# A two-layer attention and mixture-of-experts kernel: additions in two blocks of eight tiles, token transposes ahead of their rows, and the normalisation of batch 2 moved behind six scatters

## The chip, the cores and the metric

The kernel runs on one core of a Trainium2 chip. The metric is the device time of the whole program in microseconds (us), measured over several executions. TensorE (PE) multiplies matrices, VectorE (DVE) and ScalarE (ACT) work on elements, GpSimd (POOL) does small arithmetic here and issues the indirect DMAs (scatters by a list of row numbers), and SyncE (SP) issues the plain DMAs. Each engine runs its own list of instructions in order, and they wait for each other through semaphores.

## What is computed

The reference has two layers over x, four sequences (batches) of 1024 tokens with 128 features, in float32:

```python
xn = _layernorm(x)
x = x + _L0_attn_ref(xn, ...) + _L0_ffn_ref(xn, ...)   # causal attention with rotary tables; top-1 of 8 experts
xn = _layernorm(x)
x = x + _L1_attn_ref(xn, ...) + _L1_ffn_ref(xn, ...)   # long convolution (FFT) with a filter; top-2 of 8 experts
```

In the second expert layer each token goes to its two best experts: `relu(xs @ W1[e] + b1[e]) @ W2[e] + b2[e]`, weighted by the softmax of the gate logits `xn @ Wg`.

## The kernel before

Tokens are cut into 32 tiles of 128 (NT = 32, J = 8 tiles a batch). The work comes in three parts.

**The rows.** The attention of layer 0 runs as a loop over the 32 query tiles, called rows 0 to 31; PE, ACT and DVE each have a loop of their own over n. In row n PE makes the scores of tile n+1 (`scores`), transposes the probabilities of tile n (`transpose_probs`), and multiplies those of tile n-1 by the values (`weigh_values`). ACT first copies the transposes out of PSUM (`take_pt`, L1002), then takes the exponentials of tile n+1 (`exp_rows`, L992). DVE takes the maximum of tile n+1 (`row_max`, L1729), and adds the weighted values of tile n-1 to the residual (`attention_row`, L1747). In rows 20 and 22 PE also makes the rotary projections of batch 3 (`project`), whose products DVE rotates (L1721, L1722, L1712). The two PSUM banks of scores are shared by scores and projections: the second projection of row 22 waits until the exponentials of tile 22 have emptied its bank.

Hung into rows 20 to 31 is the end of layer 0 and the beginning of layer 1. `add_tiles(first, end)` on DVE adds the rows of the first expert layer to the residual (L1763), and takes the statistics of the second normalisation (L1767, L1771); `ADD_BEFORE_MAX` and `ADD_BEHIND_ROW` say in which row, ahead of `row_max` or at the row's end. POOL makes the inverse deviations out of them (`inverse_std`, L811, L813) and the negated means (L873, L875). ACT normalises the tiles of batches 0 to 2 (`norm_rows`, L1009, rows in `NORM_AT`), DVE those of batch 3 (L1502). PE transposes the normalised tiles (`transpose_norms`, L1281, four at a time, unit u covers tiles 4u to 4u+3), ACT copies them to xT (`take_transposed`, L1014), PE multiplies them by the gate weights (`gates`) and ACT copies the logits (`take_gates`, L1018), all of it in the rows of `GATES_AT`. With the logits of batches 0 and 1, which are the first half, DVE runs the routing of that half (`routing1(0, ...)`, 30 steps, L1525 to L1596) in pieces, by `ROUTING_BEFORE_MAX` and `ROUTING_BEHIND_ROW`; the tables of slots that it ends in (L1592) start the scatters. In `COUNTS_AT` PE counts the tokens of each expert; two exponentials on ACT belong to it.

**The prelude.** After row 31, PE makes the projections of layer 1 (16 units `("vu", k)`), the transposes 6 and 7 of batch 3, its gates and counts, and the eight forward transforms of the first half; DVE normalises batch 3, runs the passes of the radix step (L640 to L691), the routing of the second half and the products of the spectra (L1841). The DVE list has, in this order: normalise tiles 28 to 31, ten passes, routing up to step 12, twelve passes, the rest of the routing, eight products.

**The rounds.** 40 rounds follow, one for each pair of expert tiles: PE multiplies the two tiles of the pair, DVE adds the bias into `ys` (L1892), ACT copies the expert's weights (L1037), POOL sends the pair's rows back (`send_back`, two indirect DMAs, L849). In rounds 0 to 3 and 8 to 11 PE makes inverse transforms as well, in 4 to 7 forward ones, and behind them the output projection of the convolution. The rows of a pair are loaded by SP into 15 buffers: `load_rows` of tile n waits until tile n-15 has been sent back. Between these loads, in the same queue, SP loads the matrices of the transforms (L756).

**POOL's list**, in order: the second normalisation of batches 0, 1 and 2; the 32 dispatches of the first half (`dispatch`, L826, an indirect DMA each), with the two halves of batch 3's inverse deviations at the dispatches of `NORM_IN_SCATTER`; `SCATTER_IN_PRELUDE` dispatches of the second half; then for each pair its two `send_back` and `SCATTER_PIECES` = 2 more dispatches until all 32 are out. After every second indirect DMA POOL waits until it has been issued.

Of the kernel before, what the change touches and what calls it, by code (L numbers as in the profile page):

```python
# [168 lines left out]
GATES_AT = (23, 24, 29)  # L169
NORM_AT = {22: [(0, 0), (0, 1)], 23: [(1, 0), (1, 1)], 27: [(2, 0)], 28: [(2, 1)]}  # L170
COUNTS_AT = 26
WARM_COUNTS, WARM_FILTER, WARM_GATES, WARM_SCORES, WARM_COUNTS_2 = 7, 7, 7, {24: 3}, 6
WARM_PROBS = {5: 4, 7: 3, 9: 3, 19: 7, 22: 6, 26: 3, 28: 14}
# [5 lines left out]
ADD_BEFORE_MAX = {21: (4, 8), 22: (12, 16), 25: (20, 24), 29: (24, 28), 31: (28, 30)}  # L179
ADD_BEHIND_ROW = {20: (0, 4), 21: (8, 12), 23: (16, 20)}  # L180
ROUTING_BEFORE_MAX = {25: 6, 27: 8}
ROUTING_BEHIND_ROW = {25: 6, 26: 10, 27: R1_STEPS}
# [46 lines left out]
SCATTER_IN_PRELUDE, SCATTER_PIECES = 12, 2  # L229
NORM_IN_SCATTER = (6, 14)  # L230
# [25 lines left out]
def two_layer_kernel(nc, x_in, cst_in, rope_in, fw_in, iv_in, pe_in, wqk_in, wvg_in, w0_in, b0_in,  # L256
# [3 lines left out]
    with ctx:  # L260
# [273 lines left out]
        for n in range(NT):  # L534
            T_USES += [("p", n, c) for c in range((n % J + 4) // 4)]
# [8 lines left out]
            if gates_at(n):  # L544
                g = GATES_AT.index(n)
                T_USES += [("t", 2 * g), ("t", 2 * g + 1)]
                O_USES.append(("g", g))
# [250 lines left out]
        def _(pool):  # L798
# [70 lines left out]
            for g in range(B - 1):  # L869
# [6 lines left out]

            pool.wait_ge(ids_done, 2)
            pool.wait_ge(xn_done, NT + NT // 2)
            pool.wait_ge(slots_filled[1], 16 * TILES1 // 8)
            pool.wait_ge(slot1_ready, 2)  # L880
            for i in range(HT):
                if i in NORM_IN_SCATTER:
                    inverse_std(2 * B - 1, J // 2 * NORM_IN_SCATTER.index(i), J // 2)
                dispatch(0, 0, i)
            for g in range(2):
                second_ids(0, g)
                pool.wait_ge(ids_done, 3 + g)
                for i in range(HT // 2 * g, HT // 2 * (g + 1)):
                    dispatch(0, 1, i)
# [25 lines left out]
        def _(act):  # L915
# [125 lines left out]
            for n in range(NT):  # L1041
                take_pt(n)
# [18 lines left out]
                if gates_at(n):  # L1061
                    g = GATES_AT.index(n)
                    for u in (2 * g, 2 * g + 1):
                        take_transposed(u, t_bank("t", u))
# [80 lines left out]
        def _(pe):  # L1145
# [177 lines left out]
            for n in range(NT):  # L1323
# [6 lines left out]
                if n in FILT_AT:  # L1330
                    filter_layer(FILT_AT.index(n))
                transpose_probs(n)
# [11 lines left out]
                if gates_at(n):  # L1344
                    g = GATES_AT.index(n)
                    for u in (2 * g, 2 * g + 1):
                        wait_emptied(pe, T_USES, T_AT[("t", u)])
                        transpose_norms(u, t_bank("t", u))
                    wait_emptied(pe, O_USES, O_AT[("g", g)])
                    if g == 0:  # L1350
                        keep_running(o_bank("g", g), WARM_GATES)
# [622 lines left out]
```

## Time and profile before

| | |
|---|---|
| time, median of 3 runs (lowest to highest) | 466.6 us (465.99 to 467.1) |
| time of the profiled execution | 466.87 us |
| its span, first to last instruction | 465.0 us |
| mean granted clock of TensorE in it | 0.938 of full |
| rows 20 to 31 in it | about 156 to 232 us |
| prelude | about 232 to 274 us |
| rounds | about 274 to 450 us |

The time around the span is 1.87 us. The lines of the page and of the timeline that are used below have a section of their own. In a timeline row stand the start, the duration, the engine, the line, the operation, what it writes and reads, its shape, the number of instructions merged in it, and in brackets the idle time of the engine ahead of it with the engine and line that ended it; "issue" there means that nothing in the profile shows what ended it.

### The profile page before, as it was taken

Reading aid. Unit: us, or ns where it says so; the run is one execution under the profiler, and the core shown is the slowest. Engines: PE = TensorE matmul, PEld = TensorE weight load, DVE = VectorE, ACT = ScalarE, POOL = GpSimd, SP = SyncE. Lnnn points to the kernel's source line nnn. Section 1 sums busy time; section 2 is a strip of 40 time slices with the busy share of each in tenths; the row PEclk is TensorE's granted clock in tenths of the full one; section 3 lists DMA queues with packets and bytes.
Section 4 is the critical chain, followed back from the end, with each engine's and each line's share of the span. In section 5 each row is a group of like instructions: output and inputs, shape, how many; then the busy total and the mean of one; then the engine's idle time right before and its main releaser. Section 6 shows DMA issues by size and latency. Waiting matters only on the chain.

```text
span 465.0 us, 7797 instructions
## 1 busy us (share of the span) xinstructions
PE 369.7 (79%) x2300; PEld 297.6 (64%) x2300; DVE 289.6 (62%) x786; ACT 224.0 (48%) x551; POOL 238.2 (51%) x246
## 2 busy tenths in 40 slices
PE   0686789959999978897996989899977969777800
PEld 0662246627779646755895879898866959676700
DVE  3956635945773498387579797489439991344106
ACT  1453144213434425436253236724757886788804
POOL 3401666524666322015666566666666666565640
PEclk9998989979999989889899899999999998999965
DMA  9999999228421340001101193454341222723407
GB/s 214 280 241 327 175 172 175 58 66 277 137 68 46 91 116 1 1 0 36 42 29 41 41 243 110 122 155 137 104 130 58 79 69 74 249 84 86 126 17 260
DMA packets 64744, 55.05 MB, mean 118 GB/s; under 512 B 6819, under 2 KB 56683, under 8 KB 64446
## 3 DMA queue, kind: packets, MB, share of 16 engines
q1 hardware_dynamic: 57888, 41.71, 37.0%
q0 software_dynamic: 6656, 12.51, 8.9%
q10 hardware_dynamic: 158, 0.33, 0.4%
q8 instruction: 19, 0.31, 0.3%
q14 instruction: 23, 0.19, 0.2%
HBM read 30.44 MB, written 25.27 MB: 120 GB/s over the span
## 4 chain that ended last, share of the span: by engine, by line
PE 45%; DVE 20%; issue 12%; ACT 7%; DMA 6%; POOL 5%; SPq 2%; ACTq 1%; another core or an unknown queue 1%; POOLq 0%; DVEq 0%
PE psS L1147 22%; PE psO L1147 14%; POOL slots L839 5%; PE psT L1147 4%; DMA slots<-row,slot 3%; PE psT L1263 2%; SPq L701 2%; ACT ring L1037 1%; DVE work L1841 1%; DVE work L1729 1%; ACT row L1009 1%; DMA work<-in_wvg 1%; DVE ys L1892 1%; ACTq L1036 1%; DVE work L1855 1%
## 5 line engine op out<-in xcount | busy, mean ns | idle before, releaser
L826 POOL DMA_INDIRECT slots<-row,slot x64 | 68.0, 1063 | 46.2 <-issue 27.9
L849 POOL DMA_INDIRECT moe<-ys,xs x61 | 62.7, 1028 | 47.5 <-issue 28.0
L1037 ACT ACTIVATE ring<-w 128x642 f32 x80 | 56.1, 741 | 40.9 <-DVE ys L1892 25.3
L839 POOL DMA_INDIRECT slots<-row,slot x32 | 35.1, 1096 | 37.5 <-DVE slot L1558 19.6
L1002 ACT ACTIVATE work<-psT 128x512 f32<-128x512 f32 (+3 forms) x32 | 16.5, 515 | 69.1 <-PE psT L1263 49.4
L849 POOL DMA_INDIRECT moe<-ys,w x35 | 35.7, 1021 | 19.6 <-issue 15.8
L1147 PE MATMUL psS<-work 128*128 128x512 f32 (+3 forms) x96 | 40.8, 537 | 3.2 <-ACT w L942 1.8
L1147 PE MATMUL psO<-work 128*128 128x128 f32 x288 | 39.0, 283 | 0.0
L992 ACT ACTIVATE work<-psS,work 128x128 f32<-128x128 f32 (+7 forms) x32 | 23.6, 738 | 30.2 <-DVE work L1733 28.1
L1729 DVE TENSOR_REDUCE work<-psS 128x1 f32<-128x128 f32 (+7 forms) x32 | 24.0, 749 | 21.1 <-PE psS L1147 19.3
L1147 PE MATMUL psS<-xT,work 128*128 128x512 f32 x64 | 32.7, 656 | 5.5 <-ACT work L992 5.5
L1147 PEld LDWEIGHTS psO<-work 128*128 128x128 f32 x288 | 36.4, 200 | 0.0
L1147 PE MATMUL psS<-xT,mats 128*128 128x256 f32 x128 | 29.8, 382 | 5.1 <-issue 3.8
L1147 PE MATMUL psT<-xsT,ring 128*128 128x128 f32 x160 | 22.3, 282 | 9.8 <-ACT xsT L1102 4.7
L1147 PEld LDWEIGHTS psS<-xT,mats 128*128 128x128 f32 x128 | 23.4, 190 | 9.3 <-issue 5.0
L1147 PE MATMUL psS<-work,mats 128*128 128x256 f32 x128 | 29.0, 382 | 0.2 <-DVE work L1841 0.2
L1892 DVE TENSOR_TENSOR ys<-psS,ring 128x256 f32<-128x256 f32 x20 | 8.5, 424 | 31.8 <-PE psS L1147 17.3
L1147 PEld LDWEIGHTS psS<-work 128*128 128x128 f32 x96 | 17.4, 204 | 16.3 <-issue 8.9
L1147 PEld LDWEIGHTS psT<-xsT,ring 128*128 128x128 f32 x160 | 19.4, 191 | 12.0 <-issue 6.3
L1263 PE MATMUL psT<-cst,work 128*128 128x128 f32 x144 | 22.9, 289 | 4.9 <-ACT work L992 4.6
L1147 PEld LDWEIGHTS psS<-work,mats 128*128 128x128 f32 x128 | 24.1, 193 | 3.7 <-issue 0.6
L1147 PE MATMUL psO<-xsT,ring 128*128 128x128 f32 x160 | 22.4, 283 | 4.7 <-ACT xsT L1102 2.6
(285 smaller groups left out, 842.7 us busy)
## 6 DMA issues: line engine op xcount, KB each, us to landing
slots<-xs SPq DMA_DIRECT2D x14, 516.0 KB, 12.5
mats<-in_iv SPq DMA_DIRECT2D x16, 256.0 KB
xs<-slots SPq DMA_DIRECT2D x61, 64.5 KB
w<-in_w SPq DMA_DIRECT2D x8, 321.0 KB
w<-slots SPq DMA_DIRECT2D x35, 64.5 KB
xres<-in_x SPq DMA_DIRECT2D x4, 512.0 KB, 9.6
moe<-xs SPq DMA_DIRECT2D x4, 512.0 KB, 9.2
mats<-in_fw SPq DMA_DIRECT2D x1, 2048.0 KB, 10.3
```

What stands on the lines that cost most here:

```text
L701: sp.dma_start(xres[:, J * g:J * (g + 1), :], xv[g]).then_inc(x_loaded[g], 16)
L826: pool.indirect_dma_start(slots1[:, :], bass.IndirectOffsetOnAxis(ap=(slot1, slot2)[k][:, i:i + 1], axis=0), row[:, i, :], None, bounds_ch ...
L839: pool.indirect_dma_start(dst[:, :], bass.IndirectOffsetOnAxis(ap=slots[:, i:i + 1], axis=0), row[:, i, :], None, bounds_check=bound, oob_ ...
L849: pool.indirect_dma_start(dst[:, :], bass.IndirectOffsetOnAxis(ap=row_slots[l][m][:, D:ROWW].bitcast(I32), axis=0), ys[:, n % UNROLL, :], ...
L992: act.activation(prob[n % 2][:, 0:(i + 1) * P], S[n % 2][:, :, :].rearrange("p a m -> p (a m)")[:, 0:(i + 1) * P], ACT.Exp, bias=negmax[:, ...
L1002: act.activation(pT[n % 2][:, 0:k, :].rearrange("p j q -> p (j q)"), t_bank("p", n, 0)[:, 0:k * P], ACT.Copy).then_inc(pt_act, 1)
L1009: act.activation(row[:, i, 0:D], xres[:, i, :], ACT.Identity, bias=nbias[:, i:i + 1], scale=rstd[:, i:i + 1]).then_inc(xn_done, 1)
L1037: act.activation(pair_w[p % RING_PAIRS][:, t, :], w12[:, bass.ds(e, 1), :].rearrange("p e h -> p (e h)"), ACT.Copy).then_inc(e_w, 1)
L1147: return pe.matmul(o, lhsT, rhs, start=start, stop=stop)
L1263: last = pe.transpose(t_bank("p", n, c)[:, (j - 4 * c) * P:(j - 4 * c + 1) * P], prob[n % 2][:, j * P:(j + 1) * P], ident)
L1729: dve.tensor_reduce(negmax[:, n:n + 1], S[n % 2][:, :, :].rearrange("p a m -> p (a m)")[:, 0:(n % J + 1) * P], X, ALU.max, negate=True).th ...
L1892: tt(ys[:, m:m + 2, :], out_bank(p).rearrange("p (t d) -> p t d", d=D), pair_w[p % RING_PAIRS][:, :, B2_AT:W_COLS], ALU.add).then_inc(e_ys ...
```

## The change

On DVE, tiles 0 to 7 are added in one block behind row 20 and tiles 8 to 15 in one block ahead of the maximum in row 21; before, they were four blocks of four, in rows 20 to 22. Tiles 16 to 23, which were in rows 23 and 25, go to rows 25 and 26. The gates of batches 0 and 1 move from rows 23 and 24 to rows 22 and 23, with their token transposes now ahead of `transpose_probs` on PE and their copies ahead of `take_pt` on ACT. The normalisation of batches 0 and 1 goes to the ends of rows 21 and 22, that of batch 2 to the end of row 28 in one piece. The routing of the first half is in rows 23 (12 steps), 24 (10) and 25 (the rest, ahead of the maximum). On POOL, the second normalisation of batch 2 stands inside the scatters, ahead of dispatch 6; the two halves of batch 3 ahead of dispatches 13 and 20 (were 6 and 14). Sixteen dispatches of the second half stand ahead of the first `send_back` (were 12). Four sets of matmuls that only keep PE busy are dropped: seven ahead of the first gates, six in row 22, three in row 26 and fourteen in row 28.

```diff
-GATES_AT = (23, 24, 29)
-NORM_AT = {22: [(0, 0), (0, 1)], 23: [(1, 0), (1, 1)], 27: [(2, 0)], 28: [(2, 1)]}
-COUNTS_AT = 26
-WARM_COUNTS, WARM_FILTER, WARM_GATES, WARM_SCORES, WARM_COUNTS_2 = 7, 7, 7, {24: 3}, 6
-WARM_PROBS = {5: 4, 7: 3, 9: 3, 19: 7, 22: 6, 26: 3, 28: 14}
+TOKENS_AT = (22, 23, 29)
+GATES_AT = (22, 23, 29)
+NORM_AT = {21: [(0, 0), (0, 1)], 22: [(1, 0), (1, 1)], 28: [(2, 0), (2, 1)]}
+COUNTS_AT = 24
+WARM_COUNTS, WARM_FILTER, WARM_SCORES, WARM_COUNTS_2 = 7, 7, {24: 3}, 6
+WARM_PROBS = {5: 4, 7: 3, 9: 3, 19: 7}
...
-ADD_BEFORE_MAX = {21: (4, 8), 22: (12, 16), 25: (20, 24), 29: (24, 28), 31: (28, 30)}
-ADD_BEHIND_ROW = {20: (0, 4), 21: (8, 12), 23: (16, 20)}
-ROUTING_BEFORE_MAX = {25: 6, 27: 8}
-ROUTING_BEHIND_ROW = {25: 6, 26: 10, 27: R1_STEPS}
+ADD_BEFORE_MAX = {21: (8, 16), 26: (20, 24), 29: (24, 28), 31: (28, 30)}
+ADD_BEHIND_ROW = {20: (0, 8), 25: (16, 20)}
+ROUTING_BEFORE_MAX = {25: R1_STEPS}
+ROUTING_BEHIND_ROW = {23: 12, 24: 10}
...
-SCATTER_IN_PRELUDE, SCATTER_PIECES = 12, 2
-NORM_IN_SCATTER = (6, 14)
+SCATTER_IN_PRELUDE, SCATTER_PIECES = 16, 2
+NORM_IN_SCATTER = (6, 13, 20)
...
+            second_norm(0)
+            second_norm(1)
...
+            def norms_in_scatter(j):
+
+                if j == NORM_IN_SCATTER[0]:
+                    second_norm(2)
+                if j in NORM_IN_SCATTER[1:]:
+                    inverse_std(2 * B - 1, J // 2 * (NORM_IN_SCATTER.index(j) - 1), J // 2)
...
+                if n in TOKENS_AT:
+                    g = TOKENS_AT.index(n)
+                    for u in (2 * g, 2 * g + 1):
+                        take_transposed(u, t_bank("t", u))
                 take_pt(n)
...
+                if n in TOKENS_AT:
+                    g = TOKENS_AT.index(n)
+                    for u in (2 * g, 2 * g + 1):
+                        wait_emptied(pe, T_USES, T_AT[("t", u)])
+                        transpose_norms(u, t_bank("t", u))
                 transpose_probs(n)
```

## Rows read from the trace of the kernel before

**Rows 1.** Page: busy time of each engine, and the group of dispatches.

```profile
PE 369.7 (79%) x2300; PEld 297.6 (64%) x2300; DVE 289.6 (62%) x786; ACT 224.0 (48%) x551; POOL 238.2 (51%) x246
...
L826 POOL DMA_INDIRECT slots<-row,slot x64 | 68.0, 1063 | 46.2 <-issue 27.9
```

**Rows 2.** Timeline of POOL: dispatches (L826) and send-backs (L849).

```profile
211.13 1.12 POOL L826 DMA_INDIRECT slots<-row,slot  x1 [11.38 <-DVE slot L1592]
...
234.07 0.23 POOL L811 TENSOR_SCALAR veps<-mv 128x4 f32<-128x4 f32 x1 [1.14 <-DVE mv L1771]
...
266.00 0.97 POOL L826 DMA_INDIRECT slots<-row,slot  x1 [0.78 <-issue]
...
286.29 0.97 POOL L849 DMA_INDIRECT moe<-ys,xs  x1 [1.26 <-issue]
...
326.15 0.97 POOL L849 DMA_INDIRECT moe<-ys,w  x1 [1.00 <-issue]
...
332.97 0.97 POOL L849 DMA_INDIRECT moe<-ys,w  x1 [0.78 <-DMA slots<-row,slot]
...
397.20 0.97 POOL L849 DMA_INDIRECT moe<-ys,xs  x1 [1.93 <-DVE ys L1892]
...
448.94 0.97 POOL L849 DMA_INDIRECT moe<-ys,xs  x1 [0.30 <-issue]
```

**Rows 3.** Timeline of SP's queue and of PE in rounds 9 and 10.

```profile
331.69 1.96 PE L1147 MATMUL psS<-xT,mats 128*128 128x256 f32 x8 [0.56 <-issue]
...
337.52 0.44 SPq L756 DMA_DIRECT2D mats<-in_iv  x1
...
340.63 1.97 PE L1147 MATMUL psS<-xT,mats 128*128 128x256 f32 x8 [3.24 <-issue]
```

**Rows 4.** Stretches: busy time by engine (instructions), granted clock, DMA share, GB/s.

```profile
171.00:174.00 3.00, 3.00 (x5) 1.09 (x6) 2.69 (x12) 0.00 (x0) 0.51 (x2) 0.59 0.00 0
...
270.00:352.00 82.00, 74.67 (x458) 66.97 (x456) 55.92 (x112) 45.56 (x112) 53.33 (x51) 1.00 0.47 140
352.00:397.00 45.00, 38.63 (x311) 36.80 (x311) 32.52 (x56) 34.07 (x88) 29.07 (x26) 0.96 0.27 73
397.00:450.00 53.00, 34.09 (x269) 30.88 (x267) 15.88 (x50) 39.00 (x103) 33.20 (x34) 0.95 0.38 115
```

**Rows 5.** Timeline of DVE in rows 21 to 23.

```profile
168.51 1.06 DVE L1729 TENSOR_REDUCE work<-psS 128x1 f32<-128x896 f32 x1
...
176.60 1.13 DVE L1763 SCALAR_TENSOR_TENSOR xres<-ring,gate,xres 128x128 f32<-128x128 f32 x4
...
178.71 1.19 DVE L1729 TENSOR_REDUCE work<-psS 128x1 f32<-128x1024 f32 x1
```

**Rows 6.** Timeline of PE and ACT in rows 22 and 23.

```profile
170.94 3.21 PE L1147 MATMUL psS<-xT,work 128*128 128x512 f32 x4 [2.27 <-ACT work L992]
...
185.13 3.18 ACT L1009 ACTIVATE row<-xres,veps,rstd 128x128 f32<-128x128 f32 x8
...
188.93 1.92 PE L1147 MATMUL psO<-wg,xT 128*128 128x8 f32 x16 [1.39 <-ACT xT L1014]
```

**Rows 7.** Timeline of DVE: routing of the first half, first step and last slots.

```profile
198.32 0.37 DVE L1525 TENSOR_REDUCE m<-lg 128x16 f32<-128x128 f32 x1 [1.41 <-ACT lg L1018]
...
210.05 0.18 DVE L1592 CAST slot<-m 128x16 int32<-128x16 f32 x1
```

**Rows 8.** Timeline of POOL: the second normalisation of batch 2, first and last.

```profile
197.07 0.24 POOL L811 TENSOR_SCALAR veps<-mv 128x8 f32<-128x8 f32 x1 [15.46 <-DVE mv L1771]
...
199.49 0.25 POOL L875 TENSOR_SCALAR veps<-veps 128x8 f32<-128x8 f32 x1
```

**Rows 9.** Timeline of DVE in the prelude.

```profile
235.53 1.11 DVE L1502 TENSOR_SCALAR row<-xres,mv,rstd 128x128 f32<-128x128 f32 x4 [1.65 <-POOL rstd L813]
...
243.87 0.37 DVE L1525 TENSOR_REDUCE m<-lg 128x16 f32<-128x128 f32 x1 [0.57 <-ACT lg L1018]
...
259.04 0.17 DVE L1592 CAST slot<-m 128x16 int32<-128x16 f32 x1
```

More of the change, by code:

```diff
@@ L534, in two_layer_kernel @@
         for n in range(NT):
+            if n in TOKENS_AT:
+                T_USES += [("t", 2 * TOKENS_AT.index(n) + u) for u in range(2)]
             T_USES += [("p", n, c) for c in range((n % J + 4) // 4)]
@@ L545, in two_layer_kernel @@
                 g = GATES_AT.index(n)
-                T_USES += [("t", 2 * g), ("t", 2 * g + 1)]
                 O_USES.append(("g", g))
@@ L868, in _, with second_norm @@
             pool.tensor_copy(ids, col("token2").bitcast(I32)).then_inc(ids_done, 1)
-            for g in range(B - 1):
+            def second_norm(g):
                 tiles = slice(J * g, J * g + J)
@@ L880, in _ @@
             pool.wait_ge(slot1_ready, 2)
+            def norms_in_scatter(j):
[3 more added lines that the diff above has]
+                    inverse_std(2 * B - 1, J // 2 * (NORM_IN_SCATTER.index(j) - 1), J // 2)
             for i in range(HT):
-                if i in NORM_IN_SCATTER:
-                    inverse_std(2 * B - 1, J // 2 * NORM_IN_SCATTER.index(i), J // 2)
+                norms_in_scatter(i)
                 dispatch(0, 0, i)
@@ L888, in _ @@
                 for i in range(HT // 2 * g, HT // 2 * (g + 1)):
+                    norms_in_scatter(HT + i)
                     dispatch(0, 1, i)
@@ L1062, in _ @@
                     g = GATES_AT.index(n)
-                    for u in (2 * g, 2 * g + 1):
-                        take_transposed(u, t_bank("t", u))
                     take_gates(g, o_bank("g", g))
@@ L1331, in _ @@
                     filter_layer(FILT_AT.index(n))
+                if n in TOKENS_AT:
+                    g = TOKENS_AT.index(n)
+                    for u in (2 * g, 2 * g + 1):
+                        wait_emptied(pe, T_USES, T_AT[("t", u)])
+                        transpose_norms(u, t_bank("t", u))
                 transpose_probs(n)
@@ L1345, in _ @@
                     g = GATES_AT.index(n)
-                    for u in (2 * g, 2 * g + 1):
-                        wait_emptied(pe, T_USES, T_AT[("t", u)])
-                        transpose_norms(u, t_bank("t", u))
                     wait_emptied(pe, O_USES, O_AT[("g", g)])
-                    if g == 0:
-                        keep_running(o_bank("g", g), WARM_GATES)
                     gates(g, o_bank("g", g))
```

## The prediction

> **What bounds the kernel now.** The page's busy times name no bound: PE is busy for 79% of the span and POOL for 51% [rows 1]. So I read POOL's timeline next, because everything in layer 1's experts passes through its list. POOL starts its first dispatch at 211.13 us, and from there to the last send-back at 448.94 it has 144 indirect DMAs [rows 2]. A dispatch is shown at 1.06 us [rows 1], but the list moves by 20.3 us for the 12 dispatches from 266.00 to 286.29, that is 1.65 us each with a small wait for `ys` at the end, and by 46.7 us for seven pairs (28 DMAs) from there to the send-back of pair 7 at 332.97, 1.67 us each [rows 2]. Its shown idle time is the pace of issuing.
>
> POOL is then the bound of the first rounds, and it binds through SP: the matrices for the second transform of round 10 are queued behind the load of row tile 29, which waits until tile 14, the first of pair 7, has been sent back. Pair 7 is sent at 332.97, SP issues the matrices at 337.52, and PE starts at 340.63 after 3.24 us of idling [rows 2, 3]. The stretches show what follows. From 270 to 352 PE is busy for 74.67 of 82 us; from 352 to 397 PE (38.63), ACT (34.07) and DVE (32.52) are all near 80% of 45 us, with output projections and inverse radix passes that go by PE's and DVE's own order; from 397 to 450 PE falls to 34.09 of 53 [rows 4]. At 397.20 POOL is the one that waits, for DVE's `ys` (1.93 us idle) [rows 2]. So the end follows this chain: slots of the second half, dispatches and pairs on POOL to pair 7, PE and DVE from 340.63 to 397, POOL's last 16 pairs.
>
> **The change, part by part.**
>
> *Additions in two blocks.* Four tiles of additions with their statistics take 178.71 - 176.60 = 2.11 us of DVE [rows 5]. The block of eight ahead of row 21's maximum puts 4.2 us before `row_max(22)`, from 168.51 to 172.7 [rows 5]. The projection that waits until the exponentials of tile 22 have emptied its bank goes from 170.94 to 175.1 [rows 6]. It takes 3.21 us at a granted clock of 0.59, mostly its lower level of 1.2 GHz [rows 4, 6]. PE idled 2.3 us ahead of it and will now idle 6.4 us, so I keep the low clock. DVE's rotation shifts by the same 4.2 us, but the additions behind it are gone (-2.1), so `row_max(23)` goes from 178.71 to 180.8 [rows 5].
>
> *Transposes ahead of the row.* Behind `scores(23)`, at 180.5, PE makes units 0 and 1 and ACT empties them; by durations as in row 23 that is 1.6 us until `take_pt(22)`, 182.2. The exponentials of tile 23 end at 183.9, and the eight tiles of batch 1 (3.18 us with its tail [rows 6]) at 187.0. Units 2 and 3 are copied by 188.4, `take_pt(23)` is done at 189.0, the values of tile 22 (14 matmuls) at 190.6, the gates (1.92 us [rows 6]) at 192.5, the logits at 192.7. The routing starts then, where it started at 198.32 [rows 7]: 5.6 us earlier.
>
> *Routing in rows 23 to 25.* First step to last slots was 198.32 to 210.05, 11.7 us, with two rows in between [rows 7]. Now one row and one wait for an exponential are in between: 10.5 us. The slots are there at 203.2, and with the old distance of 1.1 us the first dispatch starts at 204.2, 6.9 us earlier.
>
> *Dropped filler matmuls.* Hidden by PE's waits if the clock holds. Lower bound 0. A stretch such as 171 to 174 at 0.59 costs 3 x 0.41 = 1.2 us [rows 4]; with two more of them the upper bound is 2.5. I take 0.
>
> *Batch 2 waits.* Its normalisation costs POOL 199.74 - 197.07 = 2.7 us [rows 8], until now spent before the slots were ready, now inside the scatters. ACT finds it done when row 28 asks for it. What stands behind it matters: dispatches 6 to 31, and both halves of batch 3. A half takes 1.4 us (POOL begins at 234.07 and DVE's wait for it ends at 235.53 [rows 2, 9]). From 211.13 to 266.00 are 54.9 us; less two halves and 1.14 us of waiting that leaves 51.0 for 32 dispatches, 1.59 each [rows 2]. Dispatch 20 is reached at 204.2 + 20 x 1.59 + 2.7 + 1.4 = 240.1, and the deviations of tiles 28 to 31 are ready at 241.5. DVE normalised them at 235.53 [rows 9]; now at 241.5, **6.0 us later**, with the passes, the second routing and the products queued behind it on DVE, and unit 7, the gates and all later transforms on PE.
>
> The rows themselves end later too: additions of eight tiles stand between the maxima of tiles 26 and 27, and row 29's eight normalisations are ahead of its transposes. By the same counting `scores(31)` starts at 225.1 for 221.9, and the prelude at 235 for 232. Its first five units end at 240.7, before DVE has normalised tiles 28 to 31, so this is covered by the wait above; 2 us more of it would not be.
>
> *The second half.* DVE was 0.6 us idle before the routing at 243.87 [rows 9]; that idling goes, and the gates (248.3) come just before the ten passes end (248.7). So slots for the second half are ready at 259.04 + 4.9 = 264.0 [rows 9]. POOL's first half ends at 204.2 + 51.0 + 2.7 + 2.8 = 260.7; it waits, and starts the second half at 265.0, where it was 266.00 [rows 2]. Of 6.9 us, 1.0 is left.
>
> *Sixteen instead of twelve.* 16 x 1.65 = 26.4, so pair 0 goes at 291.4 (286.29 before), and pair 7 at 291.4 + 46.7 = **338.1** (332.97). Four dispatches come back only behind pair 7. PE, itself 4.9 us late, has `ys` of pair 0 at 288, so no wait there.
>
> *Round 10.* From pair 7's send to PE's second transform 340.63 - 332.97 = 7.7 us passed [rows 2, 3]. From pair 6's send to the same place of round 9 it was 331.69 - 326.15 = 5.5 us. So round 10 goes on at 343.6 to 345.8: 3.0 to 5.2 us later than 340.63. I take 4.2. Without that gate PE would be 4.9 - 3.24 - 0.56 (its idling in rounds 10 and 9) [rows 3] = 1.1 us later: that is the lower bound. From there to 397 PE and DVE set the pace and nothing is given back but some waiting, which I put at 0.4; behind it 16 pairs as before.
>
> **The sum.** The profiled execution, 466.87, is 0.3 above the median. 466.6 + 4.2 - 0.4 = **470.4 us**.
>
> [...] Dispatches beside DVE's two-input operations were at 1.06 us on average [rows 1], where most in the list show 0.97 [rows 2]: a tenth more. [...]
>
> **Rivals.**
> 1. *POOL alone is the bound to the end.* Then only the start of the second half counts: 1.0 us earlier, 465.6; and were the prelude not delayed, POOL would go on at 260.7 and end up to 5 us earlier, 461.5. For it: POOL's steady pace. Against it: POOL waits for `ys` at 397.20, and PE and DVE are near 80% before [rows 2, 4]. 0.16.
> 2. *Little change.* The delay of the prelude is 1 to 3.5 us rather than 4.9, since scatters run nearer to their shown 0.97 us or row 22 is shorter, and round 10 moves by less than 1 us. 466.6. For it: PE's idling in round 10 absorbs 3.24 us [rows 3]. 0.14.
> 3. *The rows get longer.* Without filler matmuls PE's clock falls in rows 25 to 30, where PE now has 7 us of nothing to do during the routing. Each stretch like 171 to 174 costs 1.2 us [rows 4]; it decides once the prelude starts over 2 us later than 235. With three of them, 3.6 us, 1.6 pass on to POOL's second half, and with the 5.2 of round 10 that is 466.6 + 1.6 + 5.2 - 0.4 = 473.0. 0.20.
>
> The forecast has 0.50: gates and scatters as worked out, 468.5 to 472.5.
>
> **Chances and range.** The measurement tells about 0.2% (0.93 us) from no change. Faster 0.16 (rival 1), same 0.14 (rival 2), slower 0.70 (the forecast and rival 3). The range reaches to 464.8 below, into rival 1, and to 474.5 above, over rival 3 and the rule of the page.
>
> **What would show each step.** The first dispatch at 204 (203 to 206). `row_max(22)` at 172.7 and a PE gap of 6 us ahead of row 22's second projection. DVE's normalisation of tiles 28 to 31 at 241.5, ended by POOL's `rstd`. The second half's first dispatch at 265 after a wait of some 3 us for L1592. Pair 7 at 338, PE's second transform of round 10 at 343.6 to 345.8, `ys` of pair 23 near 400. The forecast is wrong if DVE normalises tiles 28 to 31 before 239, if PE in round 10 doesn't wait for matrices, or if the stretch from there to pair 23 is shorter than its 56 us, because POOL, ahead by then, had been holding it.

## The result, and the profile after

| | before | after |
|---|---|---|
| median of 20 runs, us | 466.48 | 469.67 |
| lowest to highest, us | 463.85 to 468.3 | 466.3 to 475.64 |
| profiled execution, us | 466.87 | 468.79 |
| its span, us | 465.0 | 466.9 |
| mean granted clock of TensorE in it | 0.938 | 0.933 |

After against before is 1.0061, with a 95% interval of 1.0042 to 1.0081: slower by 2 to 4 us. The forecast was 470.4. Ratios, here and below, are formed from the fast runs of each kernel (those within 1.5% of its fastest) and medians from all of its runs; on the third chip of the experiments these are 15 of before's 35 runs, with a median of 470.84 us for 473.76.

The profiled executions tell less than the medians: 1.9 us of the 3.2. A possible reason, not shown to be one: the profile of before has a wait of 3.73 us on DVE ahead of 394.37 whose releaser it can't name, and the longest such wait of after near there is 2.14 us, ahead of 396.95.

The page first: engine totals, and the dispatches as a group (instructions | busy us, mean ns | idle us ahead of them and what ended most of it).

```profile
PE 365.2 (78%) x2270; PEld 296.2 (63%) x2270; DVE 289.8 (62%) x786; ACT 223.9 (48%) x551; POOL 243.9 (52%) x246
...
L828 POOL DMA_INDIRECT slots<-row,slot x64 | 72.0, 1126 | 63.6 <-DVE slot L1606 28.8
```

Against [rows 1] PE has 30 instructions fewer (the fillers), and POOL is busy for 5.7 us more, of which the 64 dispatches have 4.0. They move the same data. One of them took 6.37 us instead of 0.97, which is more than the whole difference.

The timeline of POOL, for [rows 2] and [rows 8] (`...` stands for rows left out, in every view):

```profile
204.01 1.11 POOL L828 DMA_INDIRECT slots<-row,slot  x1 [28.82 <-DVE slot L1606]
...
212.83 0.23 POOL L813 TENSOR_SCALAR veps<-mv 128x8 f32<-128x8 f32 x1 [0.15 <-issue]
...
238.75 0.23 POOL L813 TENSOR_SCALAR veps<-mv 128x4 f32<-128x4 f32 x1 [0.15 <-issue]
...
241.83 6.37 POOL L828 DMA_INDIRECT slots<-row,slot  x1 [0.30 <-issue]
...
265.97 0.97 POOL L828 DMA_INDIRECT slots<-row,slot  x1 [0.78 <-issue]
...
292.65 1.46 POOL L851 DMA_INDIRECT moe<-ys,xs  x1 [0.78 <-issue]
...
338.22 0.97 POOL L851 DMA_INDIRECT moe<-ys,w  x1 [0.90 <-DMA slots<-row,slot]
...
399.46 0.97 POOL L851 DMA_INDIRECT moe<-ys,xs  x1 [1.15 <-DVE ys L1906]
```

The first dispatch is 7.1 us earlier than in [rows 2], and the first of the second half is where it was, 265.97 against 266.00. POOL's own list took up all of the gain: 2.7 us for batch 2's factors, and 5.4 us in dispatch 21, which took 6.37 us instead of 0.97, less the 1.1 us that POOL had waited for `mv` at 234.07 in [rows 2]. The first half had 54.9 us for its 32 dispatches before and has 62.0 now.

The timeline of DVE, for [rows 5, 7, 9]:

```profile
172.28 1.05 DVE L1743 TENSOR_REDUCE work<-psS 128x1 f32<-128x896 f32 x1
...
192.53 0.37 DVE L1539 TENSOR_REDUCE m<-lg 128x16 f32<-128x128 f32 x1 [1.65 <-ACT lg L1030]
...
202.94 0.17 DVE L1606 CAST slot<-m 128x16 int32<-128x16 f32 x1
...
240.21 1.11 DVE L1516 TENSOR_SCALAR row<-xres,mv,rstd 128x128 f32<-128x128 f32 x4 [4.58 <-POOL rstd L815]
241.24 1.22 DVE L642 TENSOR_TENSOR work<-work 128x1024 f32<-128x1024 f32 x1
...
246.66 0.68 DVE L663 SCALAR_TENSOR_TENSOR work<-work 128x512 f32<-128x512 f32 x1
247.26 0.36 DVE L1539 TENSOR_REDUCE m<-lg 128x16 f32<-128x128 f32 x1
...
262.51 0.17 DVE L1606 CAST slot<-m 128x16 int32<-128x16 f32 x1
```

DVE now waits 4.58 us for the factors of tiles 28 to 31 and normalises them at 240.21, 4.7 us later than in [rows 9]; the second half's slots are 3.5 us later. Dispatch 21 begins 0.59 us behind the first of ten radix passes, and ends 0.94 us behind the start of the reduction at 247.26 that closes their run.

The timeline of PE, for [rows 3, 6], and the stretches, for [rows 4]:

```profile
174.71 3.78 PE L1161 MATMUL psS<-xT,work 128*128 128x512 f32 x4 [6.44 <-ACT work L1004]
...
205.63 0.90 PE L1277 MATMUL psT<-cst,work 128*128 128x128 f32 x3 [6.15 <-ACT work L1004]
...
331.85 1.97 PE L1161 MATMUL psS<-xT,mats 128*128 128x256 f32 x8 [1.32 <-issue]
...
338.98 1.97 PE L1161 MATMUL psS<-xT,mats 128*128 128x256 f32 x8 [1.43 <-issue]
...
342.79 3.62 PE L1161 MATMUL psS<-xT,mats 128*128 128x256 f32 x16
...
351.32 1.97 PE L1161 MATMUL psS<-xT,mats 128*128 128x256 f32 x8 [1.19 <-issue]
```

```profile
171.00:174.00 3.00, 0.00 (x0) 0.00 (x0) 2.97 (x18) 0.44 (x1) 1.62 (x4) 0.66 0.00 0
174.00:178.00 4.00, 3.29 (x4) 1.51 (x5) 1.37 (x3) 3.73 (x10) 1.02 (x3) 0.50 0.00 0
270.00:352.00 82.00, 74.91 (x444) 66.37 (x444) 56.65 (x112) 43.18 (x107) 53.01 (x51) 1.00 0.46 139
352.00:397.00 45.00, 38.72 (x307) 36.69 (x307) 33.45 (x59) 34.38 (x87) 28.32 (x25) 0.96 0.25 65
397.00:450.00 53.00, 38.01 (x306) 34.94 (x304) 17.68 (x52) 40.87 (x109) 32.77 (x35) 0.99 0.42 123
```

PE had 34.09 us of work left behind 397 in [rows 4] and has 38.01 now: it is 4 us late, and has been since its first expert output of the second layer (its first matmuls before, then now):

```profile
281.73 1.05 PE L1147 MATMUL psO<-ring,hT 128*128 128x128 f32 x8
```

```profile
285.69 1.05 PE L1161 MATMUL psO<-ring,hT 128*128 128x128 f32 x8
```

Its waits for matrices have moved from rounds 9 and 10 to rounds 8, 9 and 11, and add up to much the same (3.8 us before, 4.5 with one of 0.59 in round 7).

Where the lateness reaches the end is seen on POOL. The groups of send-backs from the second half's start to the end, before (L849) and after (L851):

```profile
L849 POOL DMA_INDIRECT moe<-ys,xs x45 | 47.1, 1048 | 28.0 <-issue 21.7 <-DVE ys L1892 2.2 <-DMA moe<-ys,xs 1.7
L849 POOL DMA_INDIRECT moe<-ys,w x35 | 35.7, 1021 | 19.6 <-issue 15.8 <-DVE ys L1892 2.3 <-DMA slots<-row,slot 0.8
```

```profile
L851 POOL DMA_INDIRECT moe<-ys,xs x45 | 47.8, 1062 | 27.7 <-issue 21.1 <-DVE ys L1906 5.1 <-DMA moe<-ys,xs 1.5
L851 POOL DMA_INDIRECT moe<-ys,w x35 | 36.5, 1044 | 22.0 <-issue 15.3 <-DVE ys L1906 3.4 <-DMA moe<-ys,w 1.5
```

The 80 send-backs wait 49.7 us in all instead of 47.6, and the part that `ys` ends grows from 4.5 to 8.5 us. From the same start, POOL's list ends 1.9 us later (451.82 for 449.91).

### The profile page after: what moved, and what is told of

Same layout as the page of the kernel before. It is cut to its first block, busy times and chain, and to the rows that moved or that the text cites. A ratio compares the mean times of both kernels' runs of the same rounds, so it can differ in the third digit from the quotient of the medians.

```text
span 466.9 us, 7737 instructions
## 1 busy us (share of the span) xinstructions
PE 365.2 (78%) x2270; PEld 296.2 (63%) x2270; DVE 289.8 (62%) x786; ACT 223.9 (48%) x551; POOL 243.9 (52%) x246
## 4 chain that ended last, share of the span: by engine, by line
PE 33%; DVE 19%; issue 16%; POOL 10%; DMA 8%; ACT 7%; SPq 3%; ACTq 2%; POOLq 1%; another core or an unknown queue 0%; DVEq 0%
PE psS L1161 16%; PE psO L1161 9%; POOL slots L841 5%; DMA slots<-row,slot 4%; PE psT L1161 3%; POOL slots L828 3%; ACT hT L1123 2%; ACTq L1048 2%; SPq L703 2%; PE psT L1277 1%; DVE work L1855 1%; ACT ring L1049 1%; DMA moe<-ys,xs 1%; DMA work<-in_wvg 1%; DVE ys L1906 1%
## 5 line engine op out<-in xcount | busy, mean ns | idle before, releaser
L828 POOL DMA_INDIRECT slots<-row,slot x64 | 72.0, 1126 | 63.6 <-DVE slot L1606 28.8
L851 POOL DMA_INDIRECT moe<-ys,xs x61 | 63.5, 1040 | 46.2 <-issue 27.5
L841 POOL DMA_INDIRECT slots<-row,slot x32 | 35.0, 1094 | 37.7 <-DVE slot L1572 19.9
L851 POOL DMA_INDIRECT moe<-ys,w x35 | 36.5, 1044 | 22.0 <-issue 15.3
L1161 PE MATMUL psS<-work 128*128 128x512 f32 (+3 forms) x96 | 39.5, 523 | 3.2 <-ACT w L954 1.8
L1277 PEld LDWEIGHTS psT<-cst,work 128*128 128x128 f32 x144 | 17.0, 149 | 18.6 <-ACT work L1004 11.6
L1161 PEld LDWEIGHTS psS<-xT,work 128*128 128x128 f32 x64 | 13.1, 217 | 23.8 <-issue 12.9
```

The lines of the kernel that those rows point to most:

```text
L828: pool.indirect_dma_start(slots1[:, :], bass.IndirectOffsetOnAxis(ap=(slot1, slot2)[k][:, i:i + 1], axis=0), row[:, i, :], None, bounds_ch ...
L841: pool.indirect_dma_start(dst[:, :], bass.IndirectOffsetOnAxis(ap=slots[:, i:i + 1], axis=0), row[:, i, :], None, bounds_check=bound, oob_ ...
L851: pool.indirect_dma_start(dst[:, :], bass.IndirectOffsetOnAxis(ap=row_slots[l][m][:, D:ROWW].bitcast(I32), axis=0), ys[:, n % UNROLL, :], ...
L1161: return pe.matmul(o, lhsT, rhs, start=start, stop=stop)
L1277: last = pe.transpose(t_bank("p", n, c)[:, (j - 4 * c) * P:(j - 4 * c + 1) * P], prob[n % 2][:, j * P:(j + 1) * P], ident)
```

## The experiments

Twelve kernels on three chips, four on each in the order of the table, with runs of the kernel before beside them (medians 465.29, 472.11 and 473.76). Times of different chips can't be compared, so the ratios are used. A ratio can differ from the quotient of two medians; where the two disagree, both are given. Kernels of one chip are also compared directly, by their own runs.

The profiled executions differ by up to 7 us before they reach any changed code. As a mark I take DVE's pair of additions in row 20, just ahead of the first moved addition. The second table counts from there, in us.

| kernel | ratio, 95% interval | median, us |
|---|---|---|
| a_again: the changed kernel | 1.0029 (1.0003 to 1.0056) | 467.66 |
| a_inv22 | 1.0023 (0.9998 to 1.0047) | 465.92 |
| a_s12 | 1.0053 (1.0028 to 1.0079) | 467.82 |
| b_s16 | 1.0023 (0.9993 to 1.0054) | 467.13 |
| a_warm | 1.0043 (1.0009 to 1.0078) | 474.43 |
| a_norm17 | 1.0060 (1.0021 to 1.0100) | 475.17 |
| b_inv22 | 1.0015 (0.9977 to 1.0052) | 472.32 |
| a_rad4 | 1.0139 (1.0093 to 1.0184) | 477.63 |
| a_again2: the changed kernel | 1.0101 (1.0053 to 1.0149) | 476.72 |
| a_port | 1.0020 (0.9973 to 1.0068) | 474.30 |
| a_port_inv22 | 1.0025 (0.9981 to 1.0068) | 470.83 |
| a_port_inv22_s12 | 1.0082 (1.0037 to 1.0127) | 476.37 |

| from the mark | mark | first dispatch | tiles 28 to 31 | second half's slots | its first dispatch | POOL's end |
|---|---|---|---|---|---|---|
| before | 161.54 | 49.6 | 74.0 | 97.5 | 104.5 | 288.4 |
| after | 161.14 | 42.9 | 79.1 | 101.4 | 104.8 | 290.7 |
| a_again | 159.62 | 43.7 | 80.1 | 102.4 | 106.8 | 292.2 |
| a_inv22 | 159.10 | 43.8 | 80.0 | 102.3 | 105.8 | 288.8 |
| a_s12 | 160.29 | 42.8 | 79.0 | 101.3 | 105.7 | 289.4 |
| b_s16 | 160.69 | 47.6 | 72.6 | 96.2 | 103.2 | 286.6 |
| a_warm | 164.74 | 40.8 | 77.1 | 99.4 | 102.8 | 290.9 |
| a_norm17 | 166.22 | 43.0 | 76.2 | 99.9 | 103.8 | 291.3 |
| b_inv22 | 162.01 | 49.1 | 74.1 | 97.7 | 104.7 | 291.8 |
| a_rad4 | 161.18 | 43.6 | 80.1 | 104.7 | 106.0 | 296.0 |
| a_again2 | 165.51 | 42.8 | 79.0 | 101.3 | 105.7 | 293.4 |
| a_port | 163.66 | 43.1 | 79.3 | 101.8 | 103.1 | 293.8 |
| a_port_inv22 | 164.66 | 42.6 | 78.9 | 101.5 | 102.6 | 286.3 |
| a_port_inv22_s12 | 165.19 | 43.6 | 79.8 | 103.3 | 104.6 | 294.6 |

The columns up to the slots repeat within about 1 us for the same code. The last one doesn't: from the second half's start the end comes 183 to 191 us later. For the end I therefore go by the ratios.

**The change again.** Twice, unchanged.

> The changed kernel as it is, so that the others have a trace and a time of it on the same chip. Both theories: 1.005 to 1.008 of the kernel before. Its trace also tells whether the one dispatch of 6.4 us at 241.8 us in the profiled execution comes back: if it does, it belongs to the change (dispatches beside DVE's radix passes); if its longest dispatch there is under 2.5 us, it was an accident of that execution.

> The changed kernel once more, unchanged, beside the three kernels that follow on the same chip. Expected by every theory: 0.3 to 0.6% above the kernel before, the 6.37 us dispatch at GpSimd's number 21 of the first half again.

1.0029 and 1.0101, on either side of the first 1.0061, intervals of the three meeting at 1.0053 to 1.0056. Every time there is a dispatch of 6.36 us beside the radix passes (at 241.31 and at 246.11, 81.7 and 80.6 us behind the mark). Both ratios lie outside what was expected, 1.005 to 1.008 and 1.003 to 1.006, one below and one above: the size of the loss repeats less well than its sign.

**Matrices asked for earlier, in the changed kernel.** SP issues the inverse transform's matrices behind the load of tile c + 22 instead of c + 24: one pair earlier.

```diff
-INV_MATS_AFTER, FW_MATS_AFTER = 24, 16
+INV_MATS_AFTER, FW_MATS_AFTER = 22, 16
```

> The changed kernel with the inverse matrices of rounds 8 to 11 queued one pair (two row tiles) earlier on SP. Gate theory (pairs sent back on POOL hold SP's queue, and that holds PE in rounds 8 to 11): PE's waits for matrices there, 1.3 + 1.4 + 1.2 = 3.9 us in the changed kernel, are gone, and 2.5 to 3.9 us of it arrive at the end: 466 to 467 us, about 0.993 of the changed kernel. POOL theory (POOL's list alone sets the end): the waits may go, the time stays at 469.7 within 0.5. Late-prelude theory (PE itself is late and nothing else matters): stays at 469.7 within 0.5.

The waits of rounds 8 to 11 are gone (one of 1.28 us in round 7 is there instead of 0.59), which the timeline of PE shows by 16 matmuls in one piece, here for round 10:

```profile
340.72 3.62 PE L1161 MATMUL psS<-xT,mats 128*128 128x256 f32 x16
```

The median is 1.7 us below that of a_again (the means of 12 runs each differ by 1.5 us, with an uncertainty of 1.0), but the ratios, 1.0023 and 1.0029, don't tell the two apart. So the wait that my sum was built on is worth nothing by the ratios and 1.7 us by the medians; the 2.5 us or more of the gate theory did not come by either.

**The same in the kernel before.** The same one line.

> The kernel before, with the inverse transform's matrices asked for two rounds' steps earlier (as in the run with 22 in the changed kernel, which took 1.7 us off it). Theory 1 (a wait of TensorE for matrices sets the rounds' pace and so the end in both kernels): the 3.24 us wait at 340.63 goes, and the end comes 2 to 3 us earlier. Theory 2 (GpSimd's list is the floor, and TensorE had slack in the kernel before): that wait goes, the end moves by 0 to -1 us.

1.0015, no difference. The wait of 3.24 us of [rows 3] is gone: PE's transforms of round 10 start at 336.35 and those of round 11 at 341.80, 16 matmuls in one piece each. The end doesn't follow. Theory 2's forecast, 0 to 1 us less, fits and that of 2 to 3 us doesn't: the kernel before had slack behind round 10.

**Twelve dispatches ahead of the first send-back again.**

```diff
-SCATTER_IN_PRELUDE, SCATTER_PIECES = 16, 2
+SCATTER_IN_PRELUDE, SCATTER_PIECES = 12, 2
```

> The changed kernel with 12 instead of 16 dispatches ahead of the first pair. Gate theory: pair 0 goes when its ys is there, near 288 instead of 292.7, pair 7 near 334 instead of 338.2, PE waits for matrices for under 1 us in rounds 8 to 11, and the time falls by 2 to 3.5 us to about 467. POOL theory: the number of indirect DMAs is the same and POOL idles ahead of pair 0, so the time is the same or up to 2 us more, 469.7 to 471.7. Late-prelude theory: 469.7 within 0.5.

Missed: the expected gain of 2 us or more did not come (1.0053; median 0.2 us above a_again). Pair 7 went out at 333.77, that is 173.5 us behind the mark where it was 177.1 in after, and PE waited for matrices only once, 1.75 us. But POOL now came to pair 0 before its `ys` was there. The row names no releaser, but DVE ended that `ys` at 286.31, and POOL's last dispatch had ended at 285.03:

```profile
287.62 1.14 POOL L851 DMA_INDIRECT moe<-ys,xs  x1 [2.59 <-issue]
```

The four dispatches have to be issued anyway, and before pair 0 they had filled a wait. This is the edit that the prediction priced at 5 us on pair 7 and through it at 4.2 on the sum; undone, it gives nothing back (0.2 us, with an uncertainty of 1.0 for the 12 runs each).

**Sixteen in the kernel before.** The reverse edit in the other kernel.

> The kernel before with 16 instead of 12 dispatches ahead of the first pair, nothing else. Gate theory: pair 0 goes near 291.8 instead of 286.3, pair 7 near 338.5 instead of 333, PE goes on in round 10 some 3 to 5 us later, and the time is 469 to 471.5. POOL theory: the same number of DMAs and no idling ahead of pair 0 (1.26 us before), so 466 within 1. Late-prelude theory: the prelude is as before, 466.5 within 0.5.

1.0023 (0.9993 to 1.0054). Pair 7 goes 175.8 us behind the mark, where it was 171.4, and the transforms of rounds 9, 10 and 11 wait 0.46, 1.09 and 0.59 us. A send of pair 7 that is 4.4 us later costs some 1.1 us by the ratio, 1.8 by the medians, and may cost none; the gate theory had 2.5 to 5 us.

**Filler matmuls ahead of row 22's second projection.** There are 26 of them, and the first line of the edit adds 24 more ahead of row 26's transposes, so two gaps are filled and not one.

```diff
-WARM_PROBS = {5: 4, 7: 3, 9: 3, 19: 7}
+WARM_PROBS = {5: 4, 7: 3, 9: 3, 19: 7, 26: 24}
...
+                    if n == 4 * B - 1:
+                        wait_emptied(pe, T_USES, T_AT[("t", 0)])
+                        keep_running(t_bank("t", 0), 26)
```

> The changed kernel with 24 extra filler matmuls on TensorE, into the free transpose bank, just before the second projection of row 22 (the gap in which TensorE otherwise stood still for 6.44 us and came out at the low clock: that projection took 3.78 us). Theory 1 (the chain row 22, routing, first dispatch, last rstd, second half decides the end): the projection takes about 1.9 us instead of 3.8, the first dispatch comes about 1.9 us earlier (near 202.1 in a comparable execution), the second half's first dispatch 1 to 1.9 us earlier, the end 1 to 1.9 us earlier than the changed kernel's. Theory 2 (the end is set by GpSimd's list behind the second half's start, and that start by the eighth scatter-time norm and the blocked dispatch): first dispatch up to 1.9 us earlier, but the end within 0.5 us of the changed kernel's (467.7 on the chip of the earlier runs).

The stretches of this kernel and its projection:

```profile
171.00:174.00 3.00, 3.00 (x14) 1.22 (x13) 3.00 (x20) 0.00 (x0) 1.89 (x2) 1.00 0.55 165
174.00:178.00 4.00, 3.48 (x17) 1.37 (x14) 3.96 (x22) 0.84 (x1) 2.55 (x5) 1.00 0.00 0
```

```profile
178.31 1.98 PE L1161 MATMUL psS<-xT,work 128*128 128x512 f32 x4 [0.83 <-ACT work L1004]
```

With PE kept running the granted clock is 1.00, its upper level of 2.4 GHz. In after PE stood still, and the grant of 0.50 in the stretch from 174 is the lower level, 1.2 GHz. The projection takes 1.98 us instead of 3.78. The 1.8 us go through the whole chain: first dispatch, tiles 28 to 31, slots and second half's start are all 2.0 to 2.1 us earlier by the table than in after. What the fillers of row 26 add to this was not tried by itself; the first dispatch depends on rows ahead of them. The ratio is 1.0043, within the changed kernel's own on the other chips; on this one the changed kernel was not measured. Theory 1 is right on the chain and not confirmed on the end.

**Factors of tiles 28 to 31 three dispatches earlier.**

```diff
-NORM_IN_SCATTER = (6, 13, 20)
+NORM_IN_SCATTER = (6, 13, 17)
```

> The changed kernel with the norm factors of tiles 28 to 31 computed on GpSimd after dispatch 17 instead of 20 of the first half. Theory 1 (these factors are what holds VectorE back in the prelude): VectorE's normalisation of the last four tiles starts near 237.5 to 238.2 instead of 240.2, its radix passes about 2 us earlier, the slots of the second half near 260.5 instead of 262.5, the end 0.5 to 2 us earlier. Theory 2 (GpSimd's own list is the floor: 32 dispatches to 264, then 112 scatters and gathers): slots earlier by 2 us but the second half's first dispatch still at 265 to 266 and the end unchanged within 0.5 us. On the blocked dispatch: if it is tied to VectorE's run of radix passes, whichever dispatch is issued at the start of that run takes 5 to 6.5 us; if it is tied to the dispatch's own data (tile 21), it stays number 21.

Counted from the mark, the norm starts 2.9 us earlier than in after, the slots come 1.5 us earlier and the second half some 1 us; the end does not (1.0060). No dispatch took 6.4 us. Three stood beside the passes. Their rows, and those of the passes that were next to start behind the first two, are

```profile
244.66 1.67 POOL L828 DMA_INDIRECT slots<-row,slot  x1 [0.89 <-DMA slots<-row,slot]
246.63 1.43 POOL L828 DMA_INDIRECT slots<-row,slot  x1 [0.30 <-issue]
248.95 2.26 POOL L828 DMA_INDIRECT slots<-row,slot  x1 [0.89 <-DMA slots<-row,slot]
```

```profile
245.40 1.22 DVE L644 TENSOR_TENSOR work<-work 128x1024 f32<-128x1024 f32 x1
...
247.14 0.68 DVE L649 TENSOR_TENSOR work<-work 128x512 f32<-128x512 f32 x1
```

The first two end 0.93 and 0.92 us behind the start of the next pass, so the first boundary that they met let them through. The third stands over two boundaries to the end of the passes at 250.37 and ends 0.84 us behind it. So the long dispatch is not tied to number 21 or its data. It depends on how a dispatch meets the passes.

**Four passes instead of ten ahead of the second routing.**

```diff
-RADIX_FIRST = 10
+RADIX_FIRST = 4
```

> The changed kernel with four instead of ten radix passes of the second half's routing ahead of the rest (the others follow once the gates are there). Theory 1 (a GpSimd dispatch stands still for as long as VectorE runs operations with two operands in SBUF without a pause): the 6.37 us dispatch shortens to at most 3.7 us, ending when the run of four passes ends, and the six passes moved behind may block another one near 250; the second half's slots come 0 to 2 us later. Theory 2 (the long dispatch is tied to its own data or descriptors): it stays at 6.4 us. The end: 0 to +2 us by either, as the slots come no earlier.

The timelines of DVE and POOL:

```profile
245.17 0.68 DVE L649 TENSOR_TENSOR work<-work 128x512 f32<-128x512 f32 x1
248.13 0.37 DVE L1539 TENSOR_REDUCE m<-lg 128x16 f32<-128x128 f32 x1 [2.28 <-issue]
...
260.42 0.68 DVE L693 SCALAR_TENSOR_TENSOR work<-work 128x512 f32<-128x512 f32 x1
```

```profile
242.89 3.82 POOL L828 DMA_INDIRECT slots<-row,slot  x1 [0.30 <-issue]
...
258.06 3.88 POOL L828 DMA_INDIRECT slots<-row,slot  x1 [1.07 <-issue]
```

The run of four passes ends at 245.85 and the dispatch at 246.71, 0.86 us behind it; in after it was 247.34 and 248.20, again 0.86. A second dispatch of 3.88 us ends at 261.94, 0.84 behind the later run's end at 261.10. Theory 1 holds, with 3.82 us for at most 3.7: the dispatch stands as long as the run lasts. The end was dearer than either theory had it: 1.4% above before, 2 to 5 us more than the changed kernel's 0.3 to 1.0%, where 0 to 2 us were expected. This interval (from 1.0093) lies above those of a_warm and b_inv22 on the same chip and overlaps that of a_norm17. The slots come 3.3 us later than in after and PE's first expert output 4.1 us later (128.7 us behind the mark for 124.6), while POOL's second half starts no later than in a_again. So lateness of DVE and PE does reach the end; this kernel doesn't separate the two.

**The run interrupted.** Four reductions of 6 elements between the ten passes, behind passes 2, 4, 6 and 8.

```diff
+        gap = sb("gap", [P, 8])
...
-            take(passes, RADIX_FIRST)
+            for n in range(RADIX_FIRST):
+                take(passes, 1)
+                if n in (1, 3, 5, 7):
+                    dve.tensor_reduce(gap[:, n:n + 1], stats[:, 0, :], X, ALU.max)
```

> The changed kernel with four tiny one-input reductions (6 elements) between VectorE's ten radix passes at the head of the second half's routing, after passes 2, 4, 6 and 8. Theory 1 (a dispatch of GpSimd that meets a run of two-input SBUF operations of VectorE stands until the run is interrupted): the dispatch of 6.37 us shortens to at most 3.5 us, as VectorE now interrupts its run 2.3 us after its start; GpSimd's first half ends 2 to 4 us earlier, or waits for the slots at 262.5 to 263.3. If that lost time carries to the end, the end comes 1.5 to 3 us earlier than the changed kernel's; if GpSimd's list after the second half's start is lengthened by waits further on, less. Theory 2 (the long dispatch has another cause, or a gap of 0.1 us is too short for it): the dispatch stays at 6.4 us or becomes longer by the 0.4 to 0.5 us of the four reductions; the end unchanged or +0.5 us.

The timelines of DVE and of POOL:

```profile
244.01 1.22 DVE L643 TENSOR_TENSOR work<-work 128x1024 f32<-128x1024 f32 x1
...
246.28 0.15 DVE L1915 TENSOR_REDUCE gap<-stats 128x1 f32<-128x6 f32 x1
```

```profile
244.60 2.61 POOL L829 DMA_INDIRECT slots<-row,slot  x1 [0.30 <-issue]
```

The dispatch ends at 247.21, 0.93 us behind the start of the first small reduction (0.94 in after, behind the start of the large one). It takes 2.61 us instead of 6.36, for four reductions of 0.15 us on DVE. The second half's first dispatch comes 2.6 us earlier than in a_again2, from the mark. The ratio is 1.0020 against 1.0101: this is clear of a_again2 (the difference is 0.8% with some 0.7% of uncertainty; 2.4 us by the medians) but not of the changed kernel's first two measurements, 1.0061 and 1.0029. It is not faster than before.

**The same with the matrices earlier, and then also with twelve dispatches.** The one-line edits shown above, added one after the other to a_port.

> The same, and in addition the inverse transform's matrices asked for two steps earlier (22 instead of 24). Theory 1 (the blocked dispatch and TensorE's waits for matrices are the two losses, and they add): 3 to 4.5 us below the changed kernel, so 0 to 1.5 us below the kernel before. Theory 2 (GpSimd's list behind the second half's start is all that counts and that start moves by at most 1 us): 1 to 2 us below the changed kernel, as with the earlier matrices alone, and not below the kernel before.

> The same as the kernel ahead of it, with 12 instead of 16 of the first half's dispatches of the second table in the prelude (as in the kernel before). Theory 1 (the 16 put the first pair's gather and with it the transforms 4 to 5 us later, and that still costs at the end): 1 to 2 us below the kernel ahead of it. Theory 2 (all 112 operations of the list have to be issued anyway, and their order does not matter): the same within 0.5 us, as in the run with 12 alone.

The first is 1.0025 (0.9981 to 1.0068): level with the kernel before as far as this can tell. Its median of 470.83 is also that of the runs of before on which the ratio rests, 470.84. Against the changed kernel on the same chip the gain is clear by both measures: 0.8% by the ratios, with some 0.7% of uncertainty, and 5.9 us by the medians; all its 12 runs (468.11 to 473.31) lie below all 12 of a_again2 (475.27 to 481.48). Theory 1 had 3 to 4.5 us, theory 2 had 1 to 2. How much of it the matrices bring is open: against a_port 3.5 us by the medians, nothing by the ratios (1.0020 and 1.0025). And PE is as late as ever. Its first expert output starts 124.3 us behind the mark, where it was 124.6 in after and 120.2 before:

```profile
288.94 1.05 PE L1162 MATMUL psO<-ring,hT 128*128 128x128 f32 x8
```

The second was expected at or below the first. It is above: 1.0082, with an interval that overlaps the first one's, but its lowest run, 473.33, is above the highest of the first, 473.31, and the medians differ by 5.5 us. Its timeline of POOL:

```profile
286.49 0.97 POOL L829 DMA_INDIRECT slots<-row,slot  x1 [0.30 <-issue]
294.30 2.08 POOL L852 DMA_INDIRECT moe<-ys,xs  x1 [6.84 <-issue]
```

DVE ended that `ys` at 292.99. POOL stands for 6.84 us ahead of pair 0, with four dispatches behind it that it could have issued. In this kernel sixteen are better than twelve, by the single runs; by the ratios it is not shown. Both theories missed it: I had priced the position of the dispatches by what lies behind them, and not by the wait that they fill.

## Why the prediction was right, and where it was not

Slower was right, and 469.67 is near 470.4. The way there was right up to the second half's slots. Behind them the number was right for the wrong reason, and that it came so near is in part luck.

*Additions in two blocks: right.* `row_max(22)` at 172.28 for 172.7. The projection came at 174.71, behind a gap of 6.44 us for 6.4, and took 3.78 for 3.21 since it ran at the lower level throughout.

*Transposes, routing, first dispatch: right.* Routing at 192.53 for 192.7, slots at 202.94 for 203.2, first dispatch at 204.01 for 204.2.

*Dropped fillers: nearly nothing, as taken.* The prelude begins at 233.78 for 235, so rival 3 (longer rows) is out. But the wait of 6.15 us ahead of row 26's transposes shows the gap, and a_warm shows that the gap ahead of row 22's projection was worth 1.8 us on this chain, against 3.78; the kernel before had 3.21 there.

*Batch 2 on POOL: right.* 2.7 us. Tiles 28 to 31 are normalised at 240.21 for 241.5, 4.7 us later and not 6.0, since the 20 dispatches ran a little quicker than 1.59 each.

*POOL's first half: wrong by 5 us.* I had it end at 260.7 and then wait some 3 us for slots. The slots came at 262.51 for 264.0, and POOL was not there: its first half went on to 265.2. The term that failed is "32 dispatches at 1.59", and the missing 5.4 us are the one dispatch that stood through ten passes. I had spread the blocking over all dispatches, as a tenth of a us each, where it fell on one. The row did not show even that: its 1.06 us is the mean of all 64 dispatches, not of those beside two-input operations. No run shows a term of some 2 us on POOL, which the upper end of the range was to cover; what they show is the 5.4 us of one dispatch. The start at 265.97 for 265.0 looks like a hit but is the sum of two errors, -1.5 on DVE's side and +5 on POOL's.

*Sixteen dispatches and pair 7: right in time, wrong in worth.* Pair 7 at 338.22 for 338.1, PE's second transform of round 10 inside 343.6 to 345.8 (the piece that starts at 342.79 holds both transforms, 3.62 us). But "round 10 sets the rest" failed. PE waited in rounds 8, 9 and 11 instead and in round 10 not at all, which I had named as a sign against the forecast. Another sign that I had named came too: from PE's second transform of round 10, near 344.5 (half-way through its piece), to pair 23 at 399.46 it took 55 us where it had been 56.6. Taking the waits of rounds 8 to 11 away gave 1.7 us by the medians and nothing by the ratios (a_inv22), taking the 3.24 us of [rows 3] away gave nothing (b_inv22), and sending pair 7 at 333.77 gave nothing (a_s12). PE's own lateness, which with no gate was my lower bound, is in the traces: 4.0 us at the first output, 3.8 at round 10, still 4 us of work at 397. I had put it at 1.1, by letting waits absorb it that had only moved. But it is not enough by itself for a loss like that of a_again2: a_port_inv22 has the same lateness, and is 0.8% faster.

*Given back later: 0.4, wrong.* In the profiled executions 3.8 us of PE's delay become 2.3 at pair 23 and 1.9 at the end. POOL's list is close to the bound in both kernels: 112 indirect DMAs take 183 us or more from the second half's start, however early the matrices come.

*Rival 1, POOL alone.* Half right. It says that only the second half's start counts. That start didn't move, so it would have given no change. The runs with an earlier start (a_warm and a_norm17 by 1 to 2 us) show no gain at the end, a_port with 2.6 us does against a_again2, and a_rad4 shows that a late PE and DVE cost in their own right. The end needs both: POOL's list started early, and `ys` there when POOL asks.

What is shown: the 7.1 us gained at the first dispatch are spent on POOL before the second half, 2.7 by the moved factors and 5.4 by the blocked dispatch (a_rad4, a_port). With that dispatch let through and the matrices asked for earlier the changed kernel is level with before as far as the ratio tells (a_port_inv22, 1.0025 and at most 1.0068), and clear of the changed kernel on the same chip (1.0101), although the additions, the dropped fillers, the sixteen dispatches and PE's late start are all still in it. Lateness of DVE and PE costs at the end (a_rad4). Undoing the sixteen dispatches gives nothing back (a_s12, a_port_inv22_s12), though added to the kernel before they may cost 1 to 2 us (b_s16). What stays open: how the loss divides between the blocked dispatch and the matrix waits, and what PE's late start adds while these are there, which I read from the `ys` waits alone. No run brought PE's start back to where it was with the rest of the change in place.

## What to carry to other kernels

Work that is moved ahead gains only if the next queue on its way can pass the gain on: add up that queue's own list up to the point where the gain is wanted, here 32 dispatches, two or three norm factors and whatever blocks them. An instruction that waits is a price, but the same instruction in front of a wait is free; before removing or moving work on a full queue, ask what the queue would do in its place. A stall that stands in the trace just ahead of a bound need not be the bound: in the kernel before, asking for the matrices one pair earlier removed 3.24 us of PE's waiting and nothing from the time. Ask again once another loss is gone: with the dispatch let through, the kernel with the same line had the lowest median of the changed ones on its chip.

## What the runs showed of the hardware

A dispatch of GpSimd, 0.97 us by itself, could stand for as long as VectorE ran a chain of operations with two SBUF inputs, not just for the one that it met. With ten passes it took 6.36 to 6.37 us in the six traces of a changed kernel with factors at dispatch 20 and ten unbroken passes, with four passes 3.82, with the chain interrupted behind the second pass 2.61. Each time it ended 0.84 to 0.94 us behind the chain's end or the interrupting reduction's start, nearly its whole own duration. A reduction with one input of 6 elements, 0.15 us, was enough to let it through.

The Trainium skill, "SBUF — State Buffer", section "SBUF: two separate sides", says that a VectorE operation with two SBUF inputs and a GpSimd operation that reads SBUF exclude each other from a shared port for a whole instruction, whichever starts first; that GpSimd then can't write the descriptors of its DMAs it says only of VectorE's two-port modes. The trace agrees that there is a full block, and shows it for a dispatch beside two-input operations in float32. It differs in the length: dispatch 21 did not get through at the boundaries between passes, of which nine went by.

Other dispatches beside the same passes get through at the first boundary that they meet. In the kernel before two of them took 1.04 and 1.22 us, in a_norm17 two took 1.67 and 1.43, and each ended 0.92 to 0.93 us behind the start of the pass that came next. What decides is open, and the moment of arrival within a pass doesn't: the same dispatch came 0.20 us behind the start of the tenth of the twelve later passes in after and 0.21 us in a_again (255.29 for the pass), went in at the next boundary in the one and stood to the end of the chain in the other:

```profile
256.00 1.32 POOL L828 DMA_INDIRECT slots<-row,slot  x1 [0.89 <-issue]
```

```profile
255.50 2.52 POOL L828 DMA_INDIRECT slots<-row,slot  x1 [0.89 <-DMA slots<-row,slot]
```
